# Second layer's attention: the maxima are subtracted by VectorE, and ScalarE takes the exponent of a whole step at once

## The reference

```python
q = jnp.concatenate([q_c_norm, q_r], axis=-1)
k = jnp.concatenate([k_c_norm, k_r], axis=-1)
scores = jnp.einsum('bhqd,bkhd->bhqk', q, k) * scale
causal = jnp.triu(jnp.full((t, t), -jnp.inf, dtype=scores.dtype), k=1)
attn = jax.nn.softmax(scores + causal, axis=-1)
ctx = jnp.einsum('bhqk,bkhd->bhqd', attn, v_c)
out = jnp.einsum('bhtd,od->bhto', ctx, W_O)
```

## Time and profile before

| | |
|---|---|
| median of 3 runs | 1202.88 us (1201.29 to 1203.2) |
| the profiled execution's own time | 1206.21 us |
| its span | 1204.1 us |
| busy in the span: PE, DVE, ACT, POOL | 620.6, 888.5, 399.4, 392.3 us |
| the changed stage: first maxima to last copy of turned weights | 523.95 to 714.05 us |

### The profile page before, as it was taken

The page is one execution under the profiler, slowest core; times in us unless marked ns, Lnnn a source line. Parts: engine busy times, 40 slices in busy tenths (PEclk is TensorE's granted clock), DMA queues, the critical chain, the costliest instruction groups (busy, mean ns, idle before and its releaser), DMA issues. The chain is left out here.

```text
span 1204.1 us, 15402 instructions
## 1 busy us (share of the span) xinstructions
PE 620.6 (52%) x4314; PEld 480.7 (40%) x4314; DVE 888.5 (74%) x2129; ACT 399.4 (33%) x807; POOL 392.3 (33%) x404
## 2 busy tenths in 40 slices
PE   5400000000000176579999987306699999467675
PEld 3200000000000065467777765204588888334554
DVE  5898888888888975648667663155769888879485
ACT  2430100000000111455656541123166666254221
POOL 0015555555554422463455400323001111003131
PEclk9955555555555568869999998858789999778886
DMA  2000000000000000023000013110000000100000
GB/s 46 1 0 1 0 0 0 0 0 0 0 0 0 9 1 10 1 56 110 26 7 7 26 36 108 44 24 2 19 14 20 20 20 15 45 0 1 1 18 17
DMA packets 35819, 21.11 MB, mean 18 GB/s; under 512 B 8208, under 2 KB 34400, under 8 KB 35776
## 3 DMA queue, kind: packets, MB, share of 16 engines
q1 hardware_dynamic: 34752, 18.48, 5.6%
q0 software_dynamic: 1024, 2.10, 0.6%
HBM read 15.46 MB, written 5.11 MB: 17 GB/s over the span
## 5 line engine op out<-in xcount | busy, mean ns | idle before, releaser
L737 PE MATMUL l0f_gate<-xnT,l0f_w_gate 128*128 128x512 f32 x8 | 7.4, 1084 | 370.8 <-DMA l0f_w_out<-in_l_w_o 359.9
L737 PEld LDWEIGHTS l0f_gate<-xnT,l0f_w_gate 128*128 128x128 f32 x8 | 2.3, 323 | 374.8 <-DMA l0f_w_out<-in_l_w_o 360.4
L1417 DVE TENSOR_REDUCE l1a_low_top<-l1a_score 128x2 f32<-128x512 f32 (+1 forms) x96 | 66.3, 690 | 65.5 <-PE l1a_score L1297 64.3
L1385 ACT ACTIVATE l1a_weights<-l1a_score,l1a_low_top 128x128 f32<-128x128 f32 (+1 forms) x256 | 89.2, 423 | 38.3 <-DVE l1a_low_top L1417 35.1
L1251 POOL TENSOR_TENSOR l1a_q_of<-l1a_q_rows,l_quad_of 128x1024 fp32r<-128x1024 f32 x32 | 59.9, 1896 | 42.0 <-ACT l1a_q_rows L1374 42.0
L443 POOL TENSOR_TENSOR l0s_to_v<-l0s_exp_b,l_qkv 128x512 f32<-128x512 f32 x31 | 38.3, 1257 | 105.8 <-ACT l0s_exp_b L463 105.8
L2107 DVE SCALAR_TENSOR_TENSOR l2e_mixed<-l2e_down,l2e_scaled,l2e_mixed 128x128 f32<-128x128 f32 x256 | 71.7, 343 | 0.2 <-PE l2e_down L2009 0.2
L2009 PEld LDWEIGHTS l2e_down<-l2e_wd,l2e_hidden 128*128 128x128 f32 x512 | 67.2, 193 | 11.0 <-DVE l2e_hidden L2125 6.2
L2009 PE MATMUL l2e_down<-l2e_wd,l2e_hidden 128*128 128x128 f32 x512 | 69.0, 278 | 3.0 <-DVE l2e_hidden L2125 3.0
L1440 DVE COPY l1a_weightsT<-l1a_flip 128x512 f32<-128x512 f32 x96 | 65.4, 681 | 1.5 <-PE l1a_flip L1330 1.5
L1294 PE MATMUL l1a_score<-l1a_k_rows,l1a_q_of 128*128 128x128 f32 (+1 forms) x256 | 55.2, 320 | 12.1 <-ACT l1a_weights L1385 6.4
(11 more groups left out here) (438 smaller groups left out, 2059.3 us busy)
## 6 DMA issues: line engine op xcount, KB each, us to landing
l1e_w<-in_l_w SPq DMA_DIRECT2D x46, 128.0 KB, 2.1
l2e_wgu<-in_l_wgu SPq DMA_DIRECT2D x16, 128.0 KB, 2.1
l_rows<-l1r_rows SPq DMA_DIRECT2D x1, 1472.0 KB, 6.7
l_done<-l1e_done SPq DMA_DIRECT2D x23, 64.0 KB, 1.6
x_sb<-in_x SPq DMA_DIRECT2D x4, 256.0 KB, 3.7
l2e_wd<-in_l_wd SPq DMA_DIRECT2D x16, 64.0 KB, 1.8
out<-x_sb SPq DMA_DIRECT2D x8, 128.0 KB, 1.8
l3m_w<-in_l_w SPq DMA_DIRECT2D x2, 256.0 KB, 3.2
```

The lines of the kernel that those rows point to most:

```text
L1385: last = nc.scalar.activation(weights[s % 2][:, n * width:(n + 1) * width], score[s % 2][:, n * width:(n + 1) * width], ACT.Exp, bias=low_ ...
L1417: nc.vector.tensor_reduce(low_top[:, s % 2, 0:len(heads)], score[s % 2][:, :].rearrange("p (h k) -> p h k", k=key_tiles * P), AX.X, ALU.ma ...
```

## The change

The maxima are still taken by DVE. DVE then adds the negated maximum, repeated along each head's keys, to the scores, from PSUM into `weights` in SBUF, by one instruction of 512 columns. ACT takes the exponent of `weights` in place, one instruction of 512 columns for a step, with no bias. The wait for the transposes of the step two before (`flipped`) moves from ACT to DVE, ahead of the subtraction, and a wait of DVE for its own maxima is added (`order.settle`). PE's and GpSimd's lists stay as they are.

```diff
-                        if not (first and s < 2):
-                            act.wait_ge(flipped, b * STEPS + (s - 1))
                         act.wait_ge(topped, b * STEPS + (s + 1))
-                        for n in range(len(heads)):
-                            last = nc.scalar.activation(weights[s % 2][:, n * width:(n + 1) * width],
-                                                        score[s % 2][:, n * width:(n + 1) * width], ACT.Exp,
-                                                        bias=low_top[:, s % 2, n:n + 1])
-                        last.then_inc(exped, 1)
+                        nc.scalar.activation(weights[s % 2][:, :], weights[s % 2][:, :], ACT.Exp).then_inc(exped, 1)
...
-                    nc.vector.tensor_reduce(low_top[:, s % 2, 0:len(heads)],
-                                            score[s % 2][:, :].rearrange("p (h k) -> p h k", k=key_tiles * P),
-                                            AX.X, ALU.max, negate=True).then_inc(topped, 1)
+                    by_head = [x[s % 2][:, :].rearrange("p (h k) -> p h k", k=key_tiles * P) for x in (score, weights)]
+                    order.mark(nc.vector.tensor_reduce(low_top[:, s % 2, 0:len(heads)], by_head[0], AX.X, ALU.max, negate=True))
+                    if not (first and s < 2):
+                        dve.wait_ge(flipped, b * STEPS + (s - 1))
+                    order.settle()
+                    nc.vector.tensor_tensor(by_head[1], by_head[0], rep(low_top[:, s % 2, 0:len(heads)], 2, key_tiles * P),
+                                            ALU.add).then_inc(topped, 1)
...
-                    order.enter(b2, 2 * 4)
+                    order.enter(b2, 2 * (4 + STEPS))
```

More of the change, by code:

```diff
@@ L1378, in sequence @@
                     for s in range(STEPS):
-                        tile, heads, key_tiles = heads_of(s)
-                        width = key_tiles * P
-                        if not (first and s < 2):
-                            act.wait_ge(flipped, b * STEPS + (s - 1))
                         act.wait_ge(topped, b * STEPS + (s + 1))
-                        for n in range(len(heads)):
-                            last = nc.scalar.activation(weights[s % 2][:, n * width:(n + 1) * width],
-                                                        score[s % 2][:, n * width:(n + 1) * width], ACT.Exp,
-                                                        bias=low_top[:, s % 2, n:n + 1])
-                        last.then_inc(exped, 1)
+                        nc.scalar.activation(weights[s % 2][:, :], weights[s % 2][:, :], ACT.Exp).then_inc(exped, 1)
                         if s == 0 and not last_one:
@@ L1412, in _, with find_top @@
                 order = Order(dve, dve_order)
-                def find_top(b, s):
+                def find_top(b, s, first=False):
                     tile, heads, key_tiles = heads_of(s)
                     dve.wait_ge(scored, b * STEPS + (s + 1))
-                    nc.vector.tensor_reduce(low_top[:, s % 2, 0:len(heads)],
-                                            score[s % 2][:, :].rearrange("p (h k) -> p h k", k=key_tiles * P),
-                                            AX.X, ALU.max, negate=True).then_inc(topped, 1)
+                    by_head = [x[s % 2][:, :].rearrange("p (h k) -> p h k", k=key_tiles * P) for x in (score, weights)]
[5 more added lines that the diff above has]
+                                            ALU.add).then_inc(topped, 1)
                 def finish(b):
@@ L1434, in sequence @@
                         if s + 2 < STEPS:
-                            find_top(b, s + 2)
+                            find_top(b, s + 2, first)
                         elif not last_one:
@@ L1450, in sequence @@
                             route.name_tiles(order)
-                find_top(0, 0)
-                find_top(0, 1)
+                find_top(0, 0, first=True)
+                find_top(0, 1, first=True)
                 sequence(0, first=True)
                 with dve.Fori(0, B // 2 - 1) as b2:
-                    order.enter(b2, 2 * 4)
+                    order.enter(b2, 2 * (4 + STEPS))
                     sequence(b2 * 2 + 1)
```

## The result

| | kernel before | changed kernel |
|---|---|---|
| median | 1202.91 us (1201.29 to 1203.2, 4 runs) | 1222.58 us (1219.83 to 1228.32, 4 runs) |
| profiled execution, its span | 1206.21, 1204.1 us | 1221.46, 1219.7 us |
| first maxima to last finish | 523.95 to 717.71 us | 523.49 to 733.06 us |

The ratio is 1.0173, 95% interval 1.0134 to 1.0211: slower, with the whole interval above 1; whether by more or less than 2% the interval leaves open. From profile to profile it is +15.25 us, and the stage between its first maxima and its last finish has grown by 15.8 us (193.76 to 209.57), so the loss lies in the stage that was changed.

The account below looks back on a forecast made before the run. PE bounded before, and DVE was to become the bound. 9.0 + 6.5 + 0.5 made +16 us: 1222 on the profiled execution, 1219 us as median; range 1211 to 1236, likeliest case (65%) 1212 to 1224.

Parts of the forecast that it names:

- Exponents worth nothing: ACT's exponents, 96 of about 0.63 us for 256 of 423 ns: the 0.5 us saved per four-head step gains nothing.
- Subtraction 0.69 us: Each of DVE's 96 new subtractions takes 0.69 us, like the 688 ns addition of PSUM and SBUF tensors.
- Pitch 1.92: DVE's maxima, subtraction and copy, start to start, take 1.92 us a step, where it was 1.20.
- A loop batch of 24.8: Twelve steps of 1.92 plus the finish's 1.56 give 24.6 us; with tenths of DVE idle, 24.8 was taken.
- Seven batches +9.0: The batches after the first: 171.5 us for 162.5, six of 24.8 and a last of 22.7.
- Batch 0 +6.5: First batch: 14 subtractions add 10.1 us to DVE, partly filling 4.4 us of idle, 0.8 left: +6.5 us.
- The pauses +0.5: ACT takes the next batch's rows late, in four of seven batches: +3 if kept, nothing if gone, +0.5 taken.
- DVE busy +66: In the changed kernel's profile, DVE's busy time was to rise by 66 us.
- Cheap: Rival: the subtraction costs 419 ns, pitch about 0.33, PE bounds again, 1200 us; chance 4%.
- dear: Rival: the subtraction costs 1058 ns, pitch 0.97, +35 us more, 1254 us; chance 5%.
- whole-duration subtraction: Rival: DVE instructions start only after the one before ends, 2.10 us a step, 26.8 a batch, 1235 us; chance 6%.
- The rival with no lending and a longer chain: Steps lend no time, scores-to-exponents way longer, pauses kept: 25.7 us a batch, 1225 to 1230 us; chance 17%.

Follow-up runs that it names:

- act_per_head: The changed kernel with ACT's one exponent instruction a step split again into one for each head: 1223.44 us, ratio 1.0172.
- dead_in_place: The kernel before plus an unused DVE addition from PSUM in the subtraction's place, exponents still straight from the scores: 1231.98 us, ratio 1.0209.
- four_buffers: The changed kernel with four `weights` buffers, so the subtraction waits for the transposes of four steps before: 1221.96 us, ratio 1.0132.
- copy_between: The changed kernel with DVE's copy of the turned weights moved between maxima and subtraction: 1215.37 us, ratio 1.0109.
- dead instruction: The kernel before plus an unused 512-column DVE addition behind each maxima, both inputs in SBUF, no exponent waiting for it: 1237.21 us, ratio 1.0284.

## Why the prediction held

1219 us was forecast and 1222.6 measured, in the range of 1211 to 1236 and on its likeliest case. By its steps:

*Exponents worth nothing.* Right with DVE as the bound, by act_per_head. They measured 631 ns, as taken.

*Subtraction 0.69 us.* Right: 691 ns.

*Pitch 1.92.* Right in the loop, by the rows above. The gap behind R was 0.03 in 74 of the 96 steps and 0.10 in 20, all of the latter in batches 0 and 7 (532.89 to 555.10 and 706.03 to 725.32), which are written out and not in the loop. The terms for these two batches didn't foresee this.

*A loop batch of 24.8.* Right: 24.82. Part of its reason was not. I had put the 0.2 above 12 x 1.92 + 1.56 down to tenths of idle time that DVE spends on scores. The trace shows 0.2 us in a place where nothing is waited for: C at 617.66 and R at 618.45 are 0.79 apart, once a batch, just ahead of the finish. PE's heavy steps lend fully. So the size was met partly by luck: the idle tenths forecast were none, and a gap of the same size that was not forecast stood in for them.

*Seven batches +9.0.* From last copy to last copy it is 728.72 - 556.50 = 172.2 us against 162.5 in the earlier trace rows: +9.7. The six took 148.9 (last copy at 705.44) for 148.8, and the last batch 23.3, 0.6 more than the 22.7 taken, with gaps of 0.10 in place of 0.03 in ten of its steps.

*Batch 0 +6.5.* From first maxima to last copy 33.01 us against 26.88: +6.1. DVE waited 1.06 us for the third step's scores, and 0.16 twice for transposes; the rest was filled.

*The pauses +0.5.* None are seen: ACT waits before nearly every exponent now, and nothing of it reaches PE. The kernel before has some 4 us of them in its profile; they are inside the 162.5, so their going is part of the +9.7.

*The sum.* +15.25 us between the profiles where +16 was forecast: in the stage 9.7 + 6.1 = 15.8, terms that were too small and too large and offset each other. Between the medians it is +19.7. The median came out 3.6 us above the forecast because the profiled execution of before was 3.3 us above its median, and that of the changed kernel 1.1 us below its own. The changed kernel's four runs spread over 8.5 us, so these 3.6 us are no finding.

*DVE busy +66.* It rose by 58.7. The step was mis-sized: I multiplied 96 by the duration, but 0.69 us instructions that start 0.60 apart overlap in the union that the page counts; 96 x 0.61 = 58.6.

*Rivals.* Cheap, dear and whole-duration subtraction are excluded by the rows: 691 ns and 0.60 apart. The whole-duration rival took the sentence of the Trainium skill ("VectorE: DVE Perf Modes", "The DRAIN you can't avoid") more strictly than the section has it: the section also says that a next instruction that is not held starts earlier. S to C and C to R, 0.60 apart at 0.68 to 0.69, are such starts. The rival with no lending and a longer chain is not what happened here (24.82 us a batch and not 25.7, and dead_in_place, four_buffers), but in copy_between, with 0.12 us less in DVE's list per step, exponents and scores already come late. What causes ACT's pauses, and why they come in some executions only, stays open; no run was made for that.

## What to carry to other kernels

Before work is moved to an engine that idles, add up what that engine does in each step, start to start, and compare it with the bounding engine's time for the same step: here 7 us free per batch didn't carry 8.6 us of new work, and 5.8 us cost time too where they stood in a row. The free time of an average can be used only as far as the buffers let an engine run ahead, which with two is the neighbouring step. An instruction that needs the result of the one just ahead costs 0.1 to 0.2 us more than its own pitch, and reordering need not win it back: in copy_between a loop batch got 0.2 us shorter where DVE's own list promised 1.4, since scores then came late.

## What the runs showed of the hardware

DVE and GpSimd slow each other where a DVE instruction has two inputs in SBUF: 0.69 us became 1.07 beside GpSimd's L1252 and 1.63 beside L38, and four L1252 took 9.07 us (2.27 each) where they take 1.90 beside the changed kernel's subtraction, which has one input in PSUM. The Trainium skill ("SBUF — State Buffer", "SBUF: two separate sides") says that the two share a pair of ports under an exclusive lock, and that the loser blocks for the other's whole instruction. That they collide, and only with two SBUF inputs, agrees. The whole instruction does not for L1252, if the durations that the profile shows are taken for the time of the lock: dead instruction and L1252 came every 2.30 us (621.77, 624.07, 626.37, 628.67), less than 0.69 + 1.90 = 2.59. For L38 it is near: the dead instruction began 0.18 after it and lost 0.94 of the 1.09 that L38 still had to go.

The gap between R and the instruction that reads its result was 0.03 or 0.10 us for the same two operations. Which one it is went by the place in the program (loop or written out) and by the waits between them; no run separated these.
